# Spare TensorE products in five waits of a two-layer graph transformer kernel

## What is computed

```python
xn = layernorm(x)
x = x + relu(batchnorm(concat(sage(xn, src, dst), sage(xn, dst, src)))) + taylor_attention(xn)
x = x + shared_ffn(layernorm(x)) + top2_of_8_experts(layernorm(x))
xn = layernorm(x)
# linear attention: k and v are centred and scaled per head and row
dots = k^T v;  out = (q @ dots) / N;  linear = out @ w_out + b_out
x = x + sage1(relu(layernorm(xn))) + linear
x = x + slice_attention(layernorm(x))   # softmax over 64 slices per head, then sums per slice
```

## Time and profile before

| what | value |
|---|---|
| median of 3 runs (lowest, highest) | 1755.7 us (1753.57, 1757.54) |
| the profiled execution's own time | 1757.82 us |
| its span, first to last instruction | 1755.8 us |
| mean granted TensorE clock in it | 0.982 |
| stretches at half clock, windows view | ten, 64.8 us, TensorE busy in 55.3 of them |
| TensorE busy with products | 1649.4 us (94%), 9423 records |
| VectorE, ScalarE, GpSimd busy | 962.1, 669.6, 242.2 us |

### The profile page before, as it was taken

How to read it: one execution, slowest core, us unless ns; L and a number is a source line. 1 busy time by engine, 2 the same in 40 slices (tenths; PEclk the granted TensorE clock), 3 DMA queues, 4 the chain that set the end, 5 groups by cost and what they waited for, 6 DMA issues and landing times. The chain is left out here.

```text
span 1755.8 us, 31367 instructions
## 1 busy us (share of the span) xinstructions
PE 1649.4 (94%) x9423; PEld 1080.6 (62%) x9424; DVE 962.1 (55%) x2833; ACT 669.6 (38%) x1360; POOL 242.2 (14%) x290
## 2 busy tenths in 40 slices
PE   6889999998999899999999999999998989998988
PEld 5344556666667323333666899999955558644657
DVE  8899999997478663245421100000057864346962
ACT  3123455773134575666212444444423422101220
POOL 2000000002010004900063000000063111400103
PEclk9999999999999999999899999999999989999999
DMA  3001122336550000000525213221121002140001
GB/s 88 0 15 49 73 73 91 133 133 224 160 168 1 1 1 1 1 1 1 196 72 179 73 66 114 67 67 66 66 84 39 1 1 100 61 150 30 1 1 62
DMA packets 86411, 118.88 MB, mean 68 GB/s; under 512 B 6788, under 2 KB 72510, under 8 KB 86176
## 3 DMA queue, kind: packets, MB, share of 16 engines
q1 hardware_dynamic: 80992, 106.53, 18.1%
q0 software_dynamic: 3936, 10.37, 1.9%
q10 hardware_dynamic: 1376, 0.66, 0.1%
HBM read 70.66 MB, written 46.87 MB: 67 GB/s over the span
## 5 line engine op out<-in xcount | busy, mean ns | idle before, releaser
L657 PE MATMUL bank<-onehot_key,onehot_low 128*128 128x320 bf16 x1304 | 223.7, 301 | 20.0 <-DVE onehot_low L450 13.7
L446 DVE TENSOR_SCALAR onehot_key<-iota_keys,edge_keys 128x640 bf16<-128x640 f16 x652 | 230.6, 381 | 10.7 <-PE bank L657 6.1
L2002 ACT ACTIVATE hidden<-bank,b_cols 128x128 f32<-128x128 f32 x344 | 126.5, 368 | 173.9 <-PE bank L1900 150.4
L657 PEld LDWEIGHTS bank<-onehot_key,onehot_low 128*128 128x128 bf16 x1304 | 99.5, 98 | 133.6 <-DVE onehot_key L446 63.9
L2109 DVE TENSOR_TENSOR slot_columns<-bank,b_rows 128x256 f32 x43 | 18.3, 425 | 285.4 <-PE bank L1906 285.4
L1900 PEld LDWEIGHTS bank<-slot_columns,w 128*128 128x128 f32 x1376 | 160.1, 192 | 4.2 <-issue 2.2
L1900 PE MATMUL bank<-slot_columns,w 128*128 x1376 | 161.0, 275 | 1.3 <-ACT slot_columns L2010 1.3
L1906 PE MATMUL bank<-w,hidden 128*128 128x256 f32 x688 | 155.6, 379 | 0.0
L1906 PEld LDWEIGHTS bank<-w,hidden 128*128 128x128 f32 x688 | 127.4, 190 | 15.5
L523 ACT ACTIVATE edge_low_shifted<-edge_low,window_offset 128x631 f32 x81 | 66.7, 823 | 177.7 <-DVE onehot_low L450 176.0
L1616 ACT ACTIVATE XT<-bank 128x512 f32<-128x512 f32 x160 | 84.4, 602 | 60.8 <-PE bank L1544 60.8
(11 more groups left out here) (529 smaller groups left out, 2763.2 us busy)
## 6 DMA issues: line engine op xcount, KB each, us to landing
AT_dram<-at_strip SPq DMA_DIRECT2D x20, 640.0 KB, 4.7
A_dram<-a_strips SPq DMA_DIRECT2D x20, 640.0 KB, 3.0
sg_strip<-AT_dram SPq DMA_DIRECT2D x20, 640.0 KB, 4.0
back_strip<-A_dram SPq DMA_DIRECT2D x24, 480.0 KB, 6.4
w<-in_L_ffn_W1p SPq DMA_DIRECT2D x8, 1024.0 KB, 5.2
w<-in_L_ffn_W2p SPq DMA_DIRECT2D x8, 1024.0 KB, 7.8
slot_rows<-ty_zero SPq DMA_DIRECT2D x1, 6144.0 KB
slot_columns<-slot_rows SPq DMA_DIRECT2D x12, 512.0 KB, 8.7
```

The source lines that it names most:

```text
L446: dve.tensor_scalar(ohk[:, q, :], ioh[:, :], key[:, ds(chunk(n, offset, q), 1)], None, ALU.is_equal).then_inc(s_key[q], 1)
L657: last = pe.matmul(bank[2 * (x % 2) + h][:, 0:HB], ohl[q // 2][:, :, q % 2], ohk[:, q, h * HB:(h + 1) * HB], start=False, stop=q == Q - 1, ...
L2002: act.activation(hid[:, f, 0:P], bank[f % 4][:, 0:P], ACT.Gelu, bias=b1[:, ds((e + 1) * FB + f, 1)]).then_inc(s_rg, 1)
```

## The change

In five places TensorE is given extra fp32 products of 128 x 128 by 128 x 512 whose results nobody reads: 18 in all, that is 36 MATMUL records and 36 weight loads. Nothing else is changed and nothing is moved.

```diff
 # backward_stage
+                        def keep_going(n):
+                            for _ in range(n):
+                                pe.matmul(bank[5][:, :], onesf[:, :], spread(onesf[:, :], 1, WT), start=True, stop=True)
+
                         back_columns(last_cut - 1)
+                        keep_going(2)
                         back_columns(last_cut)
+                        keep_going(2)
                         squares(1)
 # experts_stage
                             if b == 2:
                                 pe.wait_ge(s_yf, WT + NB * WT)
+                                for _ in range(2):
+                                    pe.matmul(turned_bank(b, 0), onesf[:, :], la_wc[:, 0, 0:W], start=True, stop=True)
 # linear_attention_stage
+                        def keep_going(n):
+                            for _ in range(n):
+                                pe.matmul(bank[7][:, :], onesf[:, :], wc[:, 0, 0:W], start=True, stop=True)
+
                         for t in range(T):
                             if t + DEEP - 1 < T:
                                 kv(t + DEEP - 1)
+                            if t == T - 1:
+                                keep_going(3)
                             dots(t)
...
+                        keep_going(2)
                         pe.wait_ge(s_dt, 1)
...
                             turn(b)
+                        pe.wait_ge(s_xt, (NB - 1) * CB)
+                        for _ in range(2):
+                            pe.matmul(bank[TB + 3][:, :], onesf[:, :], wc[:, 0, 0:W], start=True, stop=True)
 # slice_stage
                         last.then_inc(s_tr, 1)
+                        for _ in range(5):
+                            pe.matmul(bank[3][:, :], onesf[:, :], wf[:, 0, :], start=True, stop=True)
                         for t in range(T):
```

## The result

The changed kernel took **1738.92 us**, median of five executions (1736.5 to 1745.7), beside 1753.57 (1750.4 to 1757.54, five) for the kernel before: ratio 0.9924, 95% interval 0.9898 to 0.995. The forecast, faster, came true; the time lies 1.6 us under the stated range, and the 14.7 us between the medians are more than the 11.4 of the sum. Its profiled execution took 1738.92, its span is 1737.2. One execution of the kernel before, in a later series, took 2126 us at a granted clock of 0.746 and is left out where executions are taken together.

What follows compares the result with a forecast made beforehand. TensorE's half-clock work behind long pauses, waited for by other engines, was taken as the bound. Terms 2.3, 1.1, 5.4, 1.15 and 1.45 sum to 11.4 us; between 1746.4 and 1744.3 the forecast was 1745.3 us, range 1740.5 to 1750.

Steps and rivals of the forecast that it cites:

- Batch normalisation: Sums of L809: half of TensorE's 4.62 us at half clock comes back, since VectorE waits for them: 2.3 us.
- the first products behind the switch: L1088 after the linear attention: its first 3.41 us no longer run at half clock, 1.7 us back.
- the slice attention: Its start, five products: half of 2.90 us at half clock comes back, as VectorE waits for the logits: 1.45 us.
- the linear attention's 5.4: Its tail from 1433.45 on is one chain; half of TensorE's 10.88 us at half clock comes back: 5.4 us.
- The cost of a product: Each spare product, all places: two records of 0.43 us, 0.86 us; zero-step operand at worst 0.86 a record.
- the end of a stage waits for spare products: End of the linear attention: the four records end after ScalarE, so the stage ends 0.55 us later.
- then another wait takes over: Experts' tail: the last transposes then wait for VectorE's L2143, so 1.1 us come back, not 1.7.
- the step from the sum to the time: Whole kernel: 11.4 us off the profiled execution gives 1746.4, off the median 1744.3; the middle, 1745.3 us, was taken.
- The fall moves: Clock kept up at one place falls in the next pause; one or two stretches, 1747 to 1748.7 us; chance 0.15.
- Unread products don't hold the clock: All five places: the change has no effect on the clock, 1756.3 us; chance 0.04.
- Three falls with another cause: Only linear attention and slice attention gain, 6.3 us in all, 1749.4 us; chance 0.03.
- Slower: Spare products themselves run at half clock and overrun their pauses by 13.6 us in all, 1769 us; chance 0.03.

Runs made afterwards that it cites:

- doubled kernel: The change with twice as many spare products at every place: 1754.86 us, ratio 1.0002 to the kernel before.
- one-column kernel: The change with all 18 spare products kept but streaming one column in place of 512: 1754.36 us, ratio 1.0005 to the kernel before.
- half kernel: The change with about half its spare products (2 and 0, 1, 3 and 0, 1, 2 in run order): 1746.23 us, ratio 0.9959 to the kernel before.

## Why the prediction was right and wrong

**Right: the mechanism and its sum.** All five places stand at 1.00, the forecast sum was 11.4 us and the profiles give 11.97. Batch normalisation (2.3, measured 2.27), the first products behind the switch (1.7, 1.69) and the slice attention (1.45, 1.40) are each within 0.05; the linear attention's 5.4 was 5.15, likely since half of the busy time also halves the tail of each group's last record: the first two groups take 1.16 and 1.99 us, a little over half of 2.08 and 3.78. The cost of a product holds: records start 0.43 us apart, also at zero step, where I had taken a worst case of twice that. The doubled kernel paid for overruns what the free times said.

**Right: the end of a stage waits for spare products.** 0.55 was forecast, 0.68 measured. The timeline shows the last of the four records ending at 1453.96 (1451.97 + 1.99), where ScalarE had ended at 1453.25 (1450.47 + 2.78), and the next stage starting 1.40 us after the later one. With one product the 0.68 are saved and the clock still held. That is a fault of the change that the prediction had costed but not turned round.

```profile
1450.47 2.78 ACT L2360 ACTIVATE XT<-bank,sg_gb_columns 128x512 f32<-128x512 f32 x4 [2.88 <-PE bank L2316]
...
1451.97 1.99 PE L2326 MATMUL bank<-w_kv,onesf 128*128 128x512 f32 x4 [0.23 <-ACT XT L2360]
...
1455.36 2.83 PE L1094 MATMUL bank<-sg_w,XT 128*128 128x256 f32 x12 [1.41 <-PEq L58]
```

**Wrong: the step "then another wait takes over" in the experts' tail**, 1.1 forecast, 2.14 measured. I let the last sixteen transposes of the earlier trace rows wait for VectorE's last normalised tile. They are two blocks of eight, and only the second needs it. After the change they start at 1332.27, while that tile is ready at 1332.74:

```profile
1325.30 7.13 PE L1974 MATMUL bank<-w_kv,XT 128*128 128x512 f32 x16 [0.74 <-ACT XT L2031]
...
1330.07 2.67 DVE L2151 TENSOR_SCALAR XN<-X,lnmv,lnr 128x256 f32<-128x256 f32 x8
...
1332.27 1.91 PE L1980 MATMUL bank<-ident,XN 128*128 128x128 f32 x16
```

So the whole 1.7 came back. The other 0.45 lies ahead of L1966 (6.26 us from the first transpose before, 5.81 after), in VectorE's pace: the second group of transposes waited 0.51 us for it before and 0.28 after. The kernel without these spare products had 5.87 too, so it isn't the change's.

**Wrong: the step from the sum to the time.** This is why the measured time lies outside the range. I went by a median of three executions, 1755.7; the median of 74 is 1752.9. Then I took only 10.4 from it, with the argument that the profiled execution had more half-clock work than most. It hadn't: its granted clock, 0.982, is the median of the 69 executions of the kernel before for which it is listed in the experiments. Its span is what stands out: 1755.8, where the 28 executions at 0.981 and 0.982 average 1752.1. With the sum as it stood, 1752.9 - 11.4 = 1741.5, and the 11 executions of the change have 1740.9. The first five, at 1738.9, were a low draw on top. The range's lower end allowed 3.8 us under the sum's own 1744.3 for all of this, while the executions of the kernel before alone are spread over 18 us: medians of three drawn from the 74 lie between 1750.1 and 1756.0 in eight cases of ten.

**The 6.6 us outside the five places** are some 2.4 us of clock and 3.8 us of two waits that have nothing to do with it. The clock: TensorE worked 30.1 us at half clock outside the places in the profile of before and 25.2 in that of after; half of the difference is 2.4. The waits: ahead of the batch normalisation TensorE waits for the landing of a strip from memory, and from one block of products to the next it took 5.29 us before (from 419.70) and 3.14 after (from 418.49), with the clock at 1.00 in both, which is 2.15. And in the shared experts ScalarE idles 2.86 us ahead of its last piece in before, where it idles 1.03 ahead of every other around it and in after; the profile doesn't show what it waited for ("remote"). TensorE's next product is 1.6 us later by it. Lines of before, then of after:

```profile
424.99 5.24 PE L802 MATMUL bank<-z_halves,back_strip 128*128 128x257 f16 x46 [3.46 <-DMA back_strip<-A_dram]
907.30 0.69 ACT L1994 ACTIVATE hidden<-bank,b_cols 128x512 f32<-128x512 f32 x1 [2.86 <-remote]
908.04 6.30 PE L1884 MATMUL bank<-w,hidden 128*128 128x256 f32 x21 [2.61 <-ACT hidden L1994]
```

```profile
421.63 5.57 PE L802 MATMUL bank<-z_halves,back_strip 128*128 128x257 f16 x49 [1.32 <-DMA back_strip<-A_dram]
896.45 0.69 ACT L2002 ACTIVATE hidden<-bank,b_cols 128x512 f32<-128x512 f32 x1 [1.03 <-PE bank L1884]
897.19 5.01 PE L1890 MATMUL bank<-w,hidden 128*128 128x256 f32 x22 [0.78 <-ACT hidden L2002]
```

Both are a draw: over the twelve profiles of the study the first stretch takes anything from 3.14 to 5.29 us, so these two are its extremes, and the second wait shows in the profile of before alone. Where it is the clock, an unchanged stretch takes one of a few lengths, by where the half-clock time falls: the second pass of the Taylor attention 154.80 or 157.6 to 158.1 (in the first case no fall near its start); the last stage 34.39 or 36.5 to 36.8. The shared experts' first blocks take 61.70 in before and 58.36 in the others: 1.6 of that is the wait of ScalarE, the rest the clock, which fell at 907, in this wait.

**Does the change move the other falls?** Over the executions the whole is worth what its places are worth (12.0 and 11.97). The granted clocks say the same: on average 0.9824 for the kernel before (69) and 0.9914 for the change (11), by the estimate above 61.7 and 30.1 us at half clock in each, 31.6 less, where the stretches at the five places in the earlier trace rows are 34.1 long. But the kernels with a part left out don't add up: without linear attention, switch and slice attention they are 8.2, 4.2 and 6.5 us over the change's 1740.9 (in part from different series), where the places took 4.0, 1.0 and 2.2 more, and their executions have 50, 39 and 45 us at half clock, 20, 9 and 15 more than the change, where their profiles have 10.2, 3.4 and 6.8 more at the place. Some 6 to 10 us of that lie elsewhere. Whether a place left out brings them or the series differed stays open.

**The rivals.** "The fall moves" (0.15) didn't happen at the switches; the pause of 2.25 behind the batch normalisation was passed at 1.00 in after. The profile of after does have two stretches of 3.41 us at half clock, at 575 and 950, that the one of before has not; the first shows in the kernel with the linear attention alone too, the second in the one-column kernel, so they don't need the products of the places ahead of them. The fall did move in the doubled kernel, where the clock fell at 486.7, just behind the start of the next stage. "Unread products don't hold the clock" fell, and the one-column kernel shows what would have made it true. "Three falls with another cause" fell too: with pauses filled they are gone, with one-column products they are back. Against the sentence of the Trainium skill ("TensorE: Matmul & The Clock Gate", section "Why this matters for your kernels"), which allows pauses up to about 3 us, stands the batch normalisation: one pause of 2.30 us in the half kernel, and pauses of 1.42 and 1.94 around the one-column products, and both times L809 ran at half clock for a part or all of its time, 6.04 and 6.67 us in place of 4.35. The measurement decides. "Slower" needed the clock down on entry, and it never was; its price as an overrun is the doubled kernel's 13 us.

## What to carry to other kernels

Look for stretches at half clock in the windows view before counting busy time, halve TensorE's busy time in each, and see whether the work behind it is waited for. Fill the pause ahead of it with full-width products for no more than the free time less some tenths, and one fewer where the stage ends on it; better, move real work there. And where a few stretches fall at random, take the base from dozens of executions or compare stretch by stretch between two profiles: five executions of each kernel gave 14.7 us, where the places gave 12.0. And look at what a stretch waits for before the clock is blamed: 3.8 of the 6.6 us outside the places were waits.

## What the runs showed of the hardware

The clock falls behind pauses of 2.30 us (half kernel) or of 1.42 and 1.94 us (one-column kernel), and not always: the experts' tail fell in two of three profiles without its products, and in the slice attention two products and a pause of 3.37 us were enough to stay at 1.00 once. Spare products of one column, in the same number, hold nothing. Unchanged stretches differ by 1.4 to 3.3 us between profiles from this alone, and the spread of one kernel's executions is mostly the clock: the 74 executions of the kernel before lie 18 us apart, and over the 69 for which the granted clock is listed in the experiments it accounts for 95% of the variance of the span. The 8 at 0.980 average 1754.5 us, the 13 at 0.982 average 1751.1, the 3 at 0.988 average 1742.7.
